# Routed tiles' down product in plain fp32, and expert weights loaded in 4 KB pieces

## The reference

```python
sh_mid = gelu(einsum('th,ehd->ted', xt, Wsh_up));  shared_out = einsum('ted,edh->th', sh_mid, Wsh_down)
probs = softmax(xt @ W_router);  top_v, top_i = top_k(probs, 2);  gate = one_hot(top_i) weighted by top_v
rt_mid = gelu(einsum('th,ehd->ted', xt, Wrt_up))      # 16 experts, 512 -> 256
routed_out = einsum('ted,edh->th', rt_mid * gate, Wrt_down)   # 256 -> 512
```

## Time and profile before

| | |
|---|---|
| median of 3 runs | 2127.92 us (2127.56 to 2136.31) |
| the profiled execution | 2140.55 us, of which the span is 2138.9 us |
| busy, share of the span | PE 94%, weight loads 78%, DVE 62%, ACT 39%, POOL 42% |
| mean granted TensorE clock | 0.977 of 2.4 GHz |
| DMA | 307.17 MB, 144 GB/s over the span |

### The profile page before, as it was taken

How to read it: one execution, slowest core, us unless ns; L and a number is a source line. 1 busy time by engine, 2 the same in 40 slices (tenths; PEclk the granted TensorE clock), 3 DMA queues, 4 the chain that set the end, 5 groups by cost and what they waited for, 6 DMA issues and landing times. The chain is left out here.

```text
span 2138.9 us, 29117 instructions
## 1 busy us (share of the span) xinstructions
PE 2019.6 (94%) x9877; PEld 1675.9 (78%) x9881; DVE 1329.2 (62%) x2090; ACT 843.0 (39%) x1639; POOL 890.9 (42%) x755
## 2 busy tenths in 40 slices
PE   4989999984999999999999999999989999999999
PEld 4778777773787888888888888888867888888887
DVE  7976478878677766678776666666665333333333
ACT  4533268872444444444544444444432111111111
POOL 1100023313776766667766566656641222202200
PEclk9988999997999999999999999999989999999999
DMA  7351079984666665666555555555531011000002
GB/s 282 123 212 40 16 271 384 383 291 143 193 186 193 178 187 165 180 176 192 161 165 164 144 154 167 165 157 146 165 103 30 30 30 30 20 10 29 0 1 79
DMA packets 160830, 307.17 MB, mean 144 GB/s; under 512 B 15648, under 2 KB 41120, under 8 KB 160736
## 3 DMA queue, kind: packets, MB, share of 16 engines
q1 hardware_dynamic: 144432, 251.67, 38.4%
q0 software_dynamic: 16304, 54.28, 8.0%
HBM read 210.73 MB, written 95.16 MB: 143 GB/s over the span
## 5 line engine op out<-in xcount | busy, mean ns | idle before, releaser
L1436 POOL TENSOR_TENSOR t_pT_lo<-t_pT_raw,t_pT_hi 128x512 fp32r<-128x512 f32 x256 | 328.1, 1302 | 213.7 <-ACT t_pT_hi L1552 212.1
L1660 DVE TENSOR_REDUCE t_sums<-t_score 128x1 f32<-128x512 f32 x256 | 169.6, 688 | 130.4 <-PE t_score L52 128.9
L2034 DVE TENSOR_TENSOR f_lin<-f_lin,f_silu 128x512 f32<-128x512 f32 x64 | 44.8, 700 | 290.5 <-PE f_lin L52 290.5
L1567 ACT ACTIVATE t_probs<-t_score,t_sums 128x512 f32<-128x512 f32 x256 | 175.1, 684 | 83.5 <-DVE t_sums L1660 67.4
L1650 DVE STREAM_TRANSPOSE t_blocks<-t_probs 128x512 f32<-128x512 f32 x256 | 172.8, 694 | 20.5 <-ACT t_probs L1567 20.2
L1642 DVE SCALAR_TENSOR_TENSOR x_res<-t_out,t_sums,x_res 128x512 f32<-128x512 f32 x256 | 179.5, 742 | 7.4 <-PE t_out L52 7.4
L757 POOL DMA_INDIRECT e_xg<-normalised_tokens,e_token x47 | 59.7, 1270 | 256.1 <-PE e_bank L1196 167.2
L1552 ACT ACTIVATE t_pT_hi<-t_pT_raw 128x512 fp32r<-128x512 f32 x256 | 160.1, 626 | 1.8 <-DMA t_pT_raw<-turned_blocks 1.8
L1995 ACT ACTIVATE f_silu<-f_gate 128x512 f32<-128x512 f32 x64 | 38.4, 599 | 299.0 <-PE f_gate L52 299.0
L1546 ACT ACTIVATE t_o_hi<-t_o 128x512 fp32r<-128x512 f32 x64 | 38.4, 599 | 218.1 <-PE t_o L52 218.1
L52 PE MATMUL t_score<-t_wv_hi,t_cT_hi 128*128 128x256 f32 x416 | 117.6, 283 | 0.7 <-ACT t_probs L1567 0.7
(11 more groups left out here) (338 smaller groups left out, 6008.1 us busy)
## 6 DMA issues: line engine op xcount, KB each, us to landing
turned_blocks<-t_blocks SPq DMA_DIRECT2D x256, 256.0 KB
t_pT_raw<-turned_blocks SPq DMA_DIRECT2D x256, 256.0 KB, 4.2
e_up_raw<-in_L_ffn_Wrt_up_dram SPq DMA_DIRECT2D x47, 512.0 KB
e_down_raw<-in_L_ffn_Wrt_down_dram SPq DMA_DIRECT2D x47, 512.0 KB
outputs_by_expert<-e_y_out SPq DMA_DIRECT2D x47, 256.0 KB
wq_raw<-in_L_xattn_Wq_dram POOLq DMA_DIRECT2D x32, 256.0 KB, 4.6
wk_raw<-in_L_xattn_Wk_dram POOLq DMA_DIRECT2D x32, 256.0 KB, 2.9
wv_raw<-in_L_xattn_Wv_dram POOLq DMA_DIRECT2D x16, 512.0 KB
```

Of the source, the lines that this page charges most:

```text
L1436: pool.tensor_tensor(pT_lo[:, q], pT_raw[:, q], f32(pT_hi[:, q]), ALU.subtract).then_inc(p_ready, 1)
L1567: act.activation(probs[:, t % 2, :], score_bank[t][:, :], ACT.Exp, bias=neg_max[:, t:t + 1], accum_out=inv[:, p, t:t + 1]).then_inc(exp_re ...
L1660: dve.tensor_reduce(neg_max[:, t:t + 1], score_bank[t][:, :], AX.X, ALU.max, negate=True).then_inc(max_ready, 1)
L2034: dve.tensor_tensor(lin_bank[k][:, :], lin_bank[k][:, :], silu[:, k, :], ALU.mult).then_inc(mid_done, 1)
```

## The change

The down product of the routed tiles is made in plain fp32 from down_raws and from midT, one plain copy of the turned gmid: two products of 512 columns in place of six. `split_down` on ACT and DVE and `mid_turn_lo` on DVE go. The down buffer is now read by the product itself, so its reload waits for g_down of tile i-4. The weights of the routed experts are loaded by "(p k)": partition p takes four neighbouring rows of up, or two of down, which is one piece of 4 KB in both cases. So that the sums stay the same, the transposes of xg and gmid take every fourth, or every second, column. The shared experts are not changed.

```diff
-        midT_hi, midT_lo = al.sb("midT_hi", [2, KE, P], F32R), al.sb("midT_lo", [2, KE, P], F32R)
+        midT = al.sb("midT", [2, KE, P])
...
-            up_flat = Wrt_up.rearrange("e (k p) m -> e p k m", p=P)
-            down_flat = Wrt_down.rearrange("e (k p) m -> e p k m", p=P)
+            up_flat = Wrt_up.rearrange("e (p k) m -> e p k m", p=P)
+            down_flat = Wrt_down.rearrange("e (p k) m -> e p k m", p=P)
...
                 if i < E_SH:
                     sp.wait_ge(down_ready, i + 1)
                 elif i >= RAW_RING:
-                    sp.wait_ge(down_ready, E_SH + i - RAW_RING + 1)
+                    sp.wait_ge(g_down_done, i - RAW_RING + 1)
...
-            def mid_turn_hi(n):
+            def mid_turned(n):
                 act.wait_ge(gmid_turned, n + 1)
                 if n >= 2:
                     act.wait_ge(g_down_done, n - 1)
-                act.activation(midT_hi[:, n % 2], turned_over(midT_bank[n % 2])[:, 0:KE],
-                               ACT.Copy).then_inc(midT_hi_ready, 1)
+                act.activation(midT[:, n % 2], turned_over(midT_bank[n % 2])[:, 0:KE], ACT.Copy).then_inc(midT_ready, 1)
...
             split_up(0)
             turn_hi(0)
-            split_down(0)
             split_up(1)
             turn_hi(1)
             gelu(0)
             for n in range(NSLOT):
-                mid_turn_hi(n)
+                mid_turned(n)
                 if n + 2 < NSLOT:
                     turn_hi(n + 2)
                     split_up(n + 2)
                 if n + 1 < NSLOT:
-                    split_down(n + 1)
                     gelu(n + 1)
                 out(n)
...
-            for n in range(NSLOT):
-                mid_turn_lo(n)
-                if n + 2 < NSLOT:
-                    turn_lo(n + 2)
-                    split_up(n + 2)
-                if n + 1 < NSLOT:
-                    split_down(n + 1)
+            for n in range(NSLOT - 2):
+                turn_lo(n + 2)
+                split_up(n + 2)
...
+                by_row = xg[:, n % XG_RING, :].rearrange("p (t k) -> p k t", k=KD)
                 for k in range(KD):
-                    ins = pe.transpose(xgT_bank[n % 2][:, k * P:(k + 1) * P], xg[:, n % XG_RING, k * P:(k + 1) * P],
-                                       ident[:, :])
+                    ins = pe.transpose(xgT_bank[n % 2][:, k * P:(k + 1) * P], by_row[:, k, :], ident[:, :])
...
+                by_row = gmid[:, r, :].rearrange("p (t k) -> p k t", k=KE)
                 for k in range(KE):
-                    ins = pe.transpose(midT_bank[r][:, k * P:(k + 1) * P], gmid[:, r, k * P:(k + 1) * P], ident[:, :])
+                    ins = pe.transpose(midT_bank[r][:, k * P:(k + 1) * P], by_row[:, k, :], ident[:, :])
...
             def g_down(n):
-                pe.wait_ge(down_ready, E_SH + n + 1)
+                w = n % RAW_RING
+                pe.wait_ge(down_in[w], 16 * (n // RAW_RING + 1 + (w < E_SH)))
                 pe.wait_ge(midT_ready, n + 1)
...
-                r = n % 2
-                three_pass(pe, y_bank[r][:, :], lambda k: midT_hi[:, r, k, :], lambda k: midT_lo[:, r, k, :],
-                           lambda k: down_hi[:, r, k, :], lambda k: down_lo[:, r, k, :], KE).then_inc(g_down_done, 1)
+                for k in range(KE):
+                    ins = pe.matmul(y_bank[n % 2][:, :], midT[:, n % 2, k, :], down_raws[w][:, k, :], start=(k == 0),
+                                    stop=(k == KE - 1))
+                ins.then_inc(g_down_done, 1)
```

More of the change, by code:

```diff
@@ L674, in experts_phase @@
         gmid_turned = al.sem("gmid_turned")
-        midT_hi_ready, midT_ready = al.sem("midT_hi_ready"), al.sem("midT_ready")
+        midT_ready = al.sem("midT_ready")
         g_down_done = al.sem("g_down_done")
@@ L831, in split_up @@
                 act.activation(up_hi[:, r], up_raws[w], ACT.Copy).then_inc(up_hi_ready, 1)
[L833 to L840, removed]
             def turn_hi(n):
@@ L1052, in split_up @@
                                   ALU.subtract).then_inc(up_ready, 1)
[L1054 to L1057, removed]
             def turn_lo(n):
```

## The result

| kernel | median, us | runs | ratio to before, 95% interval |
|---|---|---|---|
| before | 2127.74 (2124.94 to 2136.31) | 4 | |
| after | 2155.02 (2146.23 to 2157.38) | 4 | 1.0101 [1.007, 1.0132] |

The ratio on record is not the quotient of the two medians, which would be 1.0128. The profiled execution of after took 2154.02 us, with a span of 2152.3. The forecast was 2119.3 us, in a range of 2111 to 2128; the queues that run dry, at 2145 us, were given a chance of 0.08.

What follows compares the result with a forecast made beforehand. DMA transfers were taken to bound the routed tiles. Steady tiles -5.9, last five -1.7 and first -1.0 us sum to -8.6 us, taken from the 2127.92 us median: 2119.3 us, range 2111 to 2128.

Steps and rivals of the forecast that it cites:

- the queues that run dry: Rival: down load and store go out only after g_down(i-4), leaving DMA queues empty part of each tile; 2145 us, chance 0.08.
- The bound before: Routed tiles before the change: DMA transfers set the 4.12 us period, 0.64 us per tile above the engines alone.
- The engines' own pace: Routed tiles before the change, once loads are over: engines alone need 3.48 us per tile.
- The wait that moves: Down buffer's reload on SP, now waiting for g_down(i-4), store queued behind it: fits with 1.3 us of backlog, costs nothing.
- O + 2.4: O is the start of y_out(n); SP was to issue the store 2.4 us after it.
- The offset: Time from a y_out's start to the store's issue on SP, predicted 2.4 us.
- The landing: Time from the store's issue until the y_out it releases may start, predicted 4.2 us with empty queues.
- The 4 KB pieces: Routed weight loads at 398 GB/s: 0.16 us less per tile, -5.9 us over 37 periods, ends -2.6 and -8.1.
- PE: Routed down product: two plain fp32 products at 0.44 us each, 0.88 us instead of 1.40, -0.52 us per tile.
- The first and last tiles: Routed stage's ends, not DMA-bound: about 3.1 us per tile; -1.0 us for the first, -1.7 for the last five.
- The strided transposes: Strided weight loads of xg and gmid on PE: taken as nothing, at most 0.84 us per tile; as rival 2123.5 us, chance 0.04.
- ACT and DVE: Routed tiles after the split copies go: ACT held some 2.5 us, DVE 1.9 us per tile; neither can bound.

Runs made afterwards that it cites:

- e7: The changed kernel with six down buffers, but 1 and 2 KB pieces and contiguous transposes; median 2121.94 us, ratio to before 0.9971.
- e1: The kernel before with only the 4 KB pieces and the strided transposes they need; median 2129.25 us, ratio to before 0.9976.
- e9: The kernel before with 4 KB pieces and the store issued ahead of the down buffer's wait, rings of four; median 2122.65 us, ratio to before 0.9942.
- e8: Parts kept, 4 KB pieces, six raw buffers for up and for down, store first; median 2115.4 us, ratio to before 0.9923.
- e3: The changed kernel with the second half of the routed down product left out (output not the reference's); median 2135.76 us, one run.
- e6: The kernel before with only the down buffer's reload wait moved from down_lo(i-4) to g_down(i-4); median 2151.11 us, ratio to before 1.0091.
- e4: The changed kernel with six down buffers in place of four, so a reload waits for tile i-6; median 2114.46 us, ratio to before 0.9915.
- e10: The changed kernel with six down buffers and the store issued before the down load's wait; median 2110.9 us, ratio to before 0.9909.
- e11: The changed kernel with six down buffers and half of the down product left out (output not the reference's); median 2110.44 us, ratio to before 0.9907.
- e2: The kernel before with only the plain fp32 down product and its moved wait, short pieces, contiguous transposes; median 2150.02 us, ratio to before 1.0078.
- e5: The changed kernel, four down buffers, with the store of tile i-6 issued ahead of the wait for g_down(i-4); median 2125.97 us, ratio to before 0.9966.

## Why the prediction was wrong, point by point

**The bound before.** Right in its main reading, not complete. The transfers at 381 GB/s and a share of 1.05 set the period, but 381 is not all that this mix can do: e7 moves the same pieces at 392 GB/s, 4.01 us a tile, so some 0.1 of the 4.12 us isn't the transfers' own. But the 27.0 us that ACT waited for stores I read as their shadow alone. e1, at 4.09, shows a second limit just below, the place of the store on SP, and e9 removes it (3.87). The engines' own pace with the parts was taken too fast as well, at 3.48 us from the last tiles; the even distances of e8's and e9's first tiles are 3.63.

**The wait that moves: the step that failed.** The prediction cost it at nothing, as the store was to go out at O + 2.4 and to need 4.2 us of the 5.5 left. Both terms fell:

- *The offset*: 3.35 us in the tile shown, 3.38 in the mean, not 2.4. Nearly all of the difference is g_down, 1.95 us and not 1.03.
- *The landing*: 5.76 us, not 4.2. I had worked it from a lone store and empty queues, plus a down load and a gather. The DMA view of after (300 to 430; KB each, median us from issue to landing) has:

```profile
e_down_raw<-in_L_ffn_Wrt_down_dram SPq DMA_DIRECT2D x29, 512.0 KB, 5.4
e_up_raw<-in_L_ffn_Wrt_up_dram SPq DMA_DIRECT2D x28, 512.0 KB, 6.3
outputs_by_expert<-e_y_out SPq DMA_DIRECT2D x28, 256.0 KB, 5.7
```

An up load takes 6.3 us from issue to landing and is issued 3.4 us ahead of the store, so it is still landing for 2.9 us beside the down load. I had left it out. That this makes up the missing 1.6 us is argued; no run takes it away alone.

e3 tells the two apart. With the offset nearly as predicted, 2.60, the landing makes the period 4.31, 0.34 above my 3.97. The other 0.26 us come with the fp32 product's second half, through the offset. The offset alone, 3.38 + 4.2 = 7.58 us, would still have fitted into 7.94. By the same sum the landing alone, 2.4 + 5.76 = 8.16, makes 4.08 and takes the gain away; e3, with 0.2 us more of offset and a landing of 6.03, is already above 4.12. So the landing takes the gain, and the whole loss of 0.48 us per tile needs both. The prediction's own rule, that the cost starts when 2 x 3.97 is exceeded, was sound; e6 shows that the same loss comes without the fp32 product, as midT_lo and six products stand in its place.

**The dry queues, as a rival.** Right in place: the down load and the store go out only after g_down. Its price, 20 us from 0.55 us per tile, was close: the period rose by 0.48 and the stage by 16.8. That the queues run partly empty for some of the time is true too, but only a fine cut of the trace shows it (last section). Its sign in the profile was put wrongly: I wanted a DMA share under 0.95, and the mean is 0.97 to 0.98. And dry time added to a tile isn't how the loss comes about; the ring is.

**The 4 KB pieces.** The value taken, 398 GB/s, was too low: e4, e10 and e11 run at 411 to 413 for the mix, above even the 408 taken as the upper end for long loads alone. (Its 2.73, 2.58 and 2.51 "ms" per MB are us per MB.) The worth, 0.16 us with ends 0.07 and 0.22, holds where the transfers bind: 0.21 from e7 to e4, where PE already takes over. In the kernel before it is 0.03, and in after (4.60 against e2's 4.64) as little: the store's landing is 5.76 us in both, so the longer pieces don't shorten this ring. The Trainium skill (DMA: Bandwidth & Descriptors, the table on iDMA beside a load stream) has 408.7 GB/s, and the runs agree to 1%, though theirs is a mix with gathers and stores.

**PE.** The fp32 product was mis-sized by a factor of two: 1.72 us per tile, not 0.88. The rows were there: line 547 has 32 records for 16 products, four output tiles in each of four batches, so "eight in a row" are four products. I took a record for a product and then wrote that the trace spoke against the rule. The Trainium skill (FP8 and Floating Point Precision, TensorE Precision Notes) counts four passes for true fp32; two records of 0.43 us, each nearly twice the 0.23 of one of the three passes, agree with it, and by that rule the prediction had said 3.8 us of PE work, which is e4's period. So PE has more work with the fp32 product (four steps of 0.43 us) than with the parts (six of 0.23), and what the product saves is work on ACT and DVE, which bound nothing, and midT_lo's place ahead of g_down.

**The first and last tiles.** Wrong for the same reason. The first distances of y_out are 3.80 us (289.93, 293.73, 297.53) where before has 3.66 and 3.56, not 3.1. At the end they are (497.46 - 487.48)/3 = 3.33 where before has 3.38, not 3.14.

**The strided transposes.** The price taken, nothing, is near enough, but for the wrong reason. The weight loads of the kernel after (durations, least, median and most):

```profile
L1170 PEld LDWEIGHTS e_bank<-ident,e_xg x188: 195/207/218, 281.2 to 485.7; 128*128 128x128 f32 x188
...
L1195 PEld LDWEIGHTS e_bank<-ident,e_gmid x94: 194/210/216, 286.3 to 494.3; 128*128 128x128 f32 x94
```

The medians of 207 and 210 ns stand against 140 for xg's contiguous loads; the four transposes take 0.63 us instead of 0.60, as most of it is covered. The Trainium skill (SBUF — State Buffer, the note on SBUF "cachelines") wants two hits in a line of 16 bytes and so has gmid's stride of 8 bytes free. The row disagrees: both strides cost the same.

**ACT and DVE.** Right: 83.7 and 62.6 us of 150, and neither binds.

**What stays open.** Why e5, with four buffers, keeps some distances of up to 4.9 us that e4 lacks (stage 187.4 against 182.3); no run looked at it alone.

## What to carry to other kernels

A wait in a queue of transfers costs what stands behind it: when an edit moves a wait from an early reader to a late one, write down the ring that it closes (who waits for the transfer behind it, and who releases the wait) and take the landing times in it from loaded queues. Issue stores ahead of any load that may wait for a buffer, or give that buffer more places (two here). And before a duration in the trace is taken as the price of an instruction, count the records against the instructions of the code.

## What the runs showed of the hardware that was not expected

**A DMA share near 1 doesn't say that the queues are full.** Here are the queue rows of the loads and stores in after and in e4_ring6, 300 to 430 (packets, MB, share of 16 engines):

```profile
q1 hardware_dynamic: 12403, 37.57, 82.1%
```

```profile
q1 hardware_dynamic: 14615, 44.33, 85.1%
```

With 16 engines and 130 us that is 0.821 x 2080/37.57 = 45.5 us of an engine's time for each MB in after, and 39.9 in e4, with the same pieces. So packet time per MB is 14% longer in the kernel that issues late, and the share hardly falls (0.97 against 1.03) while the bytes fall by 16%. It isn't that all packets are slower. The packet records of the traces give a median of 0.159 us for a load's 4 KB packet in both. But 386 of 7316 such packets last over 0.3 us in after, up to 2.0, and 9 of 8683 in e4; with these few at the median, after needs 40.0 us per MB. e5, whose only difference from after is the order, has 131 of 8464, so the long packets go with the late issue; by what they become long isn't shown.

The mean share also hides holes. In half-microsecond slices of 300 to 430 us it is under 0.9 in 23% of them in after, in 2% before, in 3% in e5 and in none in e4. Two slices of the tile shown above (columns as in the earlier trace rows):

```profile
385.50:386.00 0.50, 0.24 (x3) 0.04 (x1) 0.00 (x0) 0.50 (x3) 0.11 (x1) 1.00 0.64 229
386.00:386.50 0.50, 0.46 (x1) 0.30 (x2) 0.04 (x1) 0.50 (x2) 0.00 (x0) 1.00 0.77 315
```

Read GB/s against the best that the same mix reaches, 411 to 413 here. The Trainium skill (Perfetto Trace Analysis, Identifying the Most-Contended Engine) calls the occupancy of the DMA engines misleading and goes by HBM use; these rows agree.
